# Mixing four paths on VectorE: 32 multiply-and-adds of 64 columns per half batch in place of whole weighings and additions

## The reference, cut to what matters

```
paths = (short, longp, delta, v)
probs = softmax(logits, -1); probs = maximum(probs, floor_val); probs = probs / probs.sum(-1, keepdims=True)
out = sum((probs[..., i, None] * p for i, p in enumerate(paths)))
out = out * rsqrt(mean(out * out, -1, keepdims=True) + 1e-05) * onorm_w
return out.reshape(B, L, -1) @ Wo.T
```

## Time and profile before

| | us |
|---|---|
| median of three runs | 1904.76 |
| profiled execution | 1897.1 |
| its span, first to last instruction | 1895.4 |
| VectorE busy | 1353.1 (71%) |
| TensorE busy | 1501.2 (79%) |
| ScalarE busy | 949.5 (50%) |
| GpSimd busy | 436.7 (23%) |
| mean granted TensorE clock | 0.899 of full speed |

### The profile page before, as it was taken

How to read it: one execution, slowest core, us unless ns; L and a number is a source line. 1 busy time by engine, 2 the same in 40 slices (tenths; PEclk the granted TensorE clock), 3 DMA queues, 4 the chain that set the end, 5 groups by cost and what they waited for, 6 DMA issues and landing times. The chain is left out here.

```text
span 1895.4 us, 40891 instructions
## 1 busy us (share of the span) xinstructions
PE 1501.2 (79%) x12507; PEld 1111.5 (59%) x12508; DVE 1353.1 (71%) x3875; ACT 949.5 (50%) x1998; POOL 436.7 (23%) x473
## 2 busy tenths in 40 slices
PE   6776065979999999999999999997436999999800
PEld 3446034737747657657567477476225888888700
DVE  6996055687798887887887887976455455554488
ACT  6772161356455654654655564542443555555434
POOL 6783200000030040040120310300233333333300
PEclk9997586989999999999999999987657999999955
DMA  5548632023243243333342333332524533333295
GB/s 198 191 161 256 168 72 72 3 58 100 73 119 99 60 124 102 79 90 101 93 117 81 93 100 87 93 101 63 190 99 134 188 105 103 101 105 100 79 384 192
DMA packets 297373, 224.36 MB, mean 118 GB/s; under 512 B 173472, under 2 KB 265632, under 8 KB 296960
## 3 DMA queue, kind: packets, MB, share of 16 engines
q1 hardware_dynamic: 225600, 158.84, 28.9%
q0 software_dynamic: 15232, 43.53, 6.3%
q10 hardware_dynamic: 56384, 19.93, 4.1%
HBM read 130.42 MB, written 91.82 MB: 117 GB/s over the span
## 5 line engine op out<-in xcount | busy, mean ns | idle before, releaser
L2041 POOL DMA_INDIRECT y_d<-C_yb,C_dest x136 | 131.6, 968 | 235.0 <-ACT C_yb L2152 232.6
L1465 DVE SCALAR_TENSOR_TENSOR B_conv<-B_ps_x,B_cw,B_conv 128x511 f32<-128x511 f32 (+2 forms) x192 | 143.4, 747 | 51.9 <-ACT B_conv L1177 46.9
L422 POOL DMA_INDIRECT xs_d<-x,slot_u x128 | 133.3, 1042 | 136.7 <-DVE m_acc L1867 100.0
L688 POOL MEMSET B_z<- 128x256 f32 (+4 forms) x40 | 5.6, 199 | 690.7 <-DMA B_z<-scr_a 690.7
L1177 ACT ACTIVATE B_conv<-B_ps_x,B_cw 128x512 f32<-128x512 f32 x64 | 43.7, 683 | 167.2 <-PE B_ps_x L745 165.9
L2271 DVE TENSOR_TENSOR C_av<-C_sg,C_ps_g 128x256 f32<-128x256 f32 x136 | 57.2, 421 | 95.2 <-ACT C_sg L2146 95.2
L745 PE MATMUL B_ps_x<-B_xa,B_wk 128*128 128x512 f32 x128 | 68.1, 660 | 65.8 <-DVE B_sel L1457 45.0
L2075 PE MATMUL C_ps_g<-C_w_high,C_xt_high 128*128 x272 | 120.0, 441 | 0.3 <-DVE C_xt_low L2277 0.3
L2283 DVE TENSOR_TENSOR C_avt_low<-C_ps_a,C_avt_high 128x256 fp32r<-128x256 f32 x136 | 57.6, 424 | 85.2 <-ACT C_avt_high L2141 85.2
L2075 PE MATMUL C_ps_g<-C_w_high,C_xt_low 128*128 x272 | 108.3, 398 | 0.0
L2075 PE MATMUL C_ps_g<-C_w_low,C_xt_high 128*128 x272 | 107.4, 395 | 0.0
(11 more groups left out here) (334 smaller groups left out, 4274.4 us busy)
## 6 DMA issues: line engine op xcount, KB each, us to landing
C_xb<-xs_d SPq DMA_DIRECT2D x136, 132.0 KB, 2.1
C_w_high<-y_d SPq DMA_DIRECT2D x12, 1024.0 KB, 14.0
A_band<-fir_long POOLq DMA_DIRECT2D x32, 256.0 KB, 5.6
A_work<-xT SPq DMA_DIRECT2D x16, 512.0 KB, 4.9
v_d<-A_v_tok SPq DMA_DIRECT2D x16, 512.0 KB, 3.5
short_d<-A_sh_tok SPq DMA_DIRECT2D x16, 512.0 KB, 3.2
B_xa<-xT SPq DMA_DIRECT2D x8, 1024.0 KB, 5.6
B_v_tok<-v_d SPq DMA_DIRECT2D x8, 1024.0 KB, 5.4
```

What stands on the lines that cost most here:

```text
L422: pool.indirect_dma_start(t["xs_d"][:, :], bass.IndirectOffsetOnAxis(ap=slot_u[:, c:c + 1], axis=0), x1[:, b, j, :], None).then_inc(done, 16)
L1465: V.scalar_tensor_tensor(conv[:, g % 2, k:], X[g % 2][:, :SEQ - k], cw[:, g // 4, gg % CH, 3 - k:4 - k], conv[:, g % 2, k:], ALU.mult, ALU ...
L2041: pool.indirect_dma_start(t["y_d"][:, :], bass.IndirectOffsetOnAxis(ap=dest[:, q:q + 1], axis=0), yb[:, u], None).then_inc(y_out[u], 16)
```

## The change

On VectorE a half batch is now mixed into `lo` in four steps. `weigh` multiplies the long rows as before and then joins the delta rows by 16 instructions, one for each tile and head, each of which computes `lo = rows * p + lo` on 64 columns, with the probability as a scalar per partition. `add_short` does the same with the short rows. `add_value` adds the values, weighed by ScalarE as before, in one 128 x 1024 addition. Gone are the multiplications of `delta` and `sh`, and the additions of `delta` to `lo`, of the values to `sh` and of `sh` to `lo` (the addition of the values to `lo` stands in their place). `add_value` of half 1 comes ahead of `sum_squares` of half 0; `add_rest` of half 1 came behind `scale_mix` of half 0. The semaphore `mixd` is gone, and `load_v` waits for the finished mix of both halves. The counts of `mix` stay as they were.

```diff
                 def load_v(i):
-                    hold(sp, mixd, 4 * i)
+                    for k in mix:
+                        hold(sp, k, 7 * i - 3)
                     sp.dma_start(v_tok[:], tok("v_d")[:, bass.ds(i * PT, PT), :]).then_inc(v_in, 16)
...
+                def add_weighed(i, b, rows, k):
+                    for j in range(TPB):
+                        for h in range(HEADS):
+                            n_, hs = b * TPB + j, slice(h * DH, (h + 1) * DH)
+                            w = V.scalar_tensor_tensor(lo[:, b, j, hs], rows[:, j, hs],
+                                                       lg[:, n_ * HEADS + h, k:k + 1], lo[:, b, j, hs],
+                                                       ALU.mult, ALU.add)
+                    w.then_inc(mix[b], 1)
                 def weigh(i, b):
...
                     dve.wait_ge(sm_dve, 11 * (i + 1))
-                    V.tensor_tensor(v3(lo[:, b]), v3(lo[:, b]), p3(1), ALU.mult).then_inc(mix[b], 1)
-                    V.tensor_tensor(v3(dlt), v3(dlt), p3(2), ALU.mult).then_inc(mix[b], 1)
-                    V.tensor_tensor(v3(sh[:, b]), v3(sh[:, b]), p3(0), ALU.mult).then_inc(mixd, 1)
-                def add_two(i, b):
+                    V.tensor_tensor(v3(lo[:, b]), v3(lo[:, b]), long_p, ALU.mult).then_inc(mix[b], 1)
+                    dve.wait_ge(mix[b], 7 * i + 1)
+                    add_weighed(i, b, delta[:, b * TPB:(b + 1) * TPB], 2)
+                def add_short(i, b):
                     dve.wait_ge(mix[b], 7 * i + 2)
-                    V.tensor_tensor(lo[:, b], lo[:, b], delta[:, b * TPB:(b + 1) * TPB], ALU.add).then_inc(mix[b], 1)
-                    val = v_tok[:, b * TPB:(b + 1) * TPB]
-                    dve.wait_ge(mixd, 2 * (2 * i + b) + 1)
+                    add_weighed(i, b, sh[:, b], 0)
+                def add_value(i, b):
+                    dve.wait_ge(mix[b], 7 * i + 3)
                     dve.wait_ge(weighed, 2 * i + b + 1)
-                    V.tensor_tensor(sh[:, b], sh[:, b], val, ALU.add).then_inc(mixd, 1)
-                def add_rest(i, b):
-                    dve.wait_ge(mix[b], 7 * i + 3)
-                    dve.wait_ge(mixd, 2 * (2 * i + b + 1))
-                    V.tensor_tensor(lo[:, b], lo[:, b], sh[:, b], ALU.add).then_inc(mix[b], 1)
+                    V.tensor_tensor(lo[:, b], lo[:, b], v_tok[:, b * TPB:(b + 1) * TPB], ALU.add).then_inc(mix[b], 1)
...
                         merge(i + 1, 0)
-                    add_two(i, 0)
-                    add_rest(i, 0)
+                    add_short(i, 0)
+                    add_value(i, 0)
                     if has_next:
                         merge(i + 1, 1)
                     weigh(i, 1)
                     if has_next:
                         merge(i + 1, 2)
-                    add_two(i, 1)
+                    add_short(i, 1)
+                    add_value(i, 1)
                     sum_squares(i, 0)
                     if has_next:
                         merge(i + 1, 3)
                     scale_mix(i, 0)
-                    add_rest(i, 1)
                     sum_squares(i, 1)
```

More of the change, by code:

```diff
@@ L514, in delta_and_gate @@
         sm_dve, sm_exp = sem("softmax_dve"), sem("softmax_exp")
-        weighed, mixd, mix = sem("values_weighed"), sem("mix_rest"), [sem(f"mix_dve{i}") for i in range(2)]
+        weighed, mix = sem("values_weighed"), [sem(f"mix_dve{i}") for i in range(2)]
         sq_ok, rms_rt = sem("rms_squared"), sem("rms_rooted")
@@ L1724, in weigh @@
                 def weigh(i, b):
-                    p3 = lambda k: lg[:, 16 * b:16 * b + 16, k:k + 1].to_broadcast([P, 16, DH])
-                    dlt = delta[:, b * TPB:(b + 1) * TPB]
+                    long_p = lg[:, 16 * b:16 * b + 16, 1:2].to_broadcast([P, 16, DH])
                     dve.wait_ge(sm_dve, 11 * (i + 1))
-                    V.tensor_tensor(v3(lo[:, b]), v3(lo[:, b]), p3(1), ALU.mult).then_inc(mix[b], 1)
-                    V.tensor_tensor(v3(dlt), v3(dlt), p3(2), ALU.mult).then_inc(mix[b], 1)
```

## The result

| | before | after |
|---|---|---|
| median of the runs, us | 1902.93 (4 runs) | 1928.93 (4 runs) |
| ratio to before, 95% interval | | 1.0144 (1.0116 to 1.0172) |
| profiled execution, us | 1897.1 | 1928.5 |
| span, us | 1895.4 | 1926.8 |
| VectorE busy, us | 1353.1 | 1388.5 |

The two profiled executions lie 31.4 us apart: the one of the kernel before is 6 us faster than the median of its runs, the other at its median.

The account below looks back on a forecast made before the run. VectorE was taken to set the end of a pair's mixing, with TensorE waiting. Seven pairs at 2.4 us plus 2.6 in the last gave +19 on 1904.8: 1924 us, by itself 1916 to 1932, all cases 1908 to 1940.

Parts of the forecast that it names:

- The instruction: VectorE's added 64-column multiply-and-adds start 0.195 us apart, sixteen last 3.2 us; +1.7 us of work per half batch.
- The rule of the Trainium skill: 58 cycles plus columns at 0.96 GHz, 127 ns for 64 columns; weighed against 0.195 us, it would give the faster rival's sum.
- The weighing of half 0, hidden in the gap: VectorE's first weighing grows to 4.46 us, cost 0: hidden by 1.0 of the 1.63 us gap ahead of the taps.
- Short rows of half 0 behind GpSimd's masking: On VectorE, the first short-row multiply-and-add waits for GpSimd's masking to end, as the long addition did; cost +0.9 us.
- The order gives back the wait for the square: On VectorE, the 1.12 us wait ahead of the second sum of squares goes; reordering gives back 2.3 of 4.0 us.
- `first_rows` waits about 0.7 us for the load: Values' load lands 4.0 us later, at 864.3; VectorE reaches `first_rows` at 863.6 and waits about 0.7 us.
- L937 moves by 2.4 us a pair: TensorE's L937, behind `first_rows` and merge 4 at the mixing's end, moves from 863.92 to 866.3: +2.4 us.
- The last pair: No merges, no load, no gap hiding the first weighing: its second sum of squares comes 2.6 us later.
- TensorE in between, at no cost: TensorE's L929 starts 2.2 us later and ends at 864.4, in time for merge 4: cost 0.
- The clock: Rival, 12%: another stretch at TensorE's lower clock after new idling, 1.7 us a pair, 12 us more: 1936 us.
- The last rival: 10%: half or more of the step meets slack in the recurrence, where VectorE waits for TensorE's products: 1905 to 1914.

Follow-up runs that it names:

- the run with a constant: The changed kernel with the constant 0.25 in place of each row's probability in the 64-column multiply-and-adds: 1893.66 us, ratio 0.9934 to the kernel before.
- the order alone: The kernel before with its instructions kept and half 1's last addition moved ahead of half 0's sum of squares: 1887.57 us, ratio 0.9911.
- the instructions alone: The changed kernel in the old order, half 1's values added behind the scaling of half 0: 1953.1 us, ratio 1.0294 to the kernel before.
- the values first: The changed kernel with half 1's values added ahead of its short rows, the next values' load waiting for that addition alone: by itself 1923.86 us, ratio 1.0104.
- the first filler alone: The changed kernel with two more TensorE filler products ahead of L930, VectorE's program untouched: 1925.35 us, ratio 1.0098 to the kernel before.

## Why the prediction was right, and where its sum fell short

*The instruction* (forecast 0.195 us apart, 3.2 us for sixteen): right, 0.196 and 3.22. The whole cost hung on choosing the row of the same operation with a scalar per partition over the row of equally short statistics; the run with a constant shows that this scalar is what sets the two apart. The rule of the Trainium skill ("VectorE: DVE Perf Modes", section on the TRN2 errata) that was weighed there, by which 64 columns are an estimate of 127 ns, is met by the constant's 0.136 us more nearly than by the 0.196 us of this kernel.

*The weighing of half 0, hidden in the gap:* right, 1.63 became 0.57. *Short rows of half 0 behind GpSimd's masking:* right, the call at 854.85 takes 4.21 us, 1.0 more than elsewhere. The masking in that mixing:

```profile
852.21 3.83 POOL L699 TENSOR_SCALAR_AFFINE_SELECT area<-area 128x4096 f32<-128x4096 f32 x1 [12.43 <-DMA area<-scr_xt]
```

In the first pair the masking (GpSimd, below) falls into the delta rows' call (VectorE) instead:

```profile
433.93 3.98 POOL L699 TENSOR_SCALAR_AFFINE_SELECT area<-area 128x4096 f32<-128x4096 f32 x1 [35.80 <-DMA area<-scr_xt]
```
```profile
431.12 6.87 DVE L1730 SCALAR_TENSOR_TENSOR B_lo<-B_delta,B_lg,B_lo 128x64 f32<-128x64 f32 x16
```

6.87 us in place of 3.22. The prediction did not look at where the masking lies in that pair. In the kernel before it starts 4.2 us behind the mixing's start there (437.98 - 433.82), 6.1 in the pair that was followed. VectorE's busy time grew by 35 us where 27 were forecast; the held call is 3.7 us of that.

*The order gives back the wait for the square:* right, and confirmed from both sides by the order alone and the instructions alone. *`first_rows` waits about 0.7 us for the load:* right, 0.73. *L937 moves by 2.4 us a pair:* 2.52 in the pair that was followed, but there luck helped: the other six moved by 3.1 to 6.2 us, and the seven by 3.8 on average. *The last pair:* right, its second sum of squares comes 2.46 us later after the mixing's start (20.85 us against 18.39), where 2.6 were forecast.

*TensorE in between, at no cost:* this is the step that failed, a term of the sum put at 0. The prediction saw L929 start 2.2 us late (2.38 measured, 873.65 - 846.14 against 858.31 - 833.18) and counted it as covered because VectorE was later still. The idling was followed by a longer stretch at 1.2 GHz, some 10 us in place of 3.4 in that pair: L930 itself grew from 3.94 to 5.71 us, which the prediction had at 3.94. In the profiled executions, the parts from `first_rows` on are 5.6 + 8.3 = 13.9 us over seven mixings, where the sum has 0. The part up to `first_rows` is 20.8 us, where the sum has 7 x 2.4 = 16.8; 2.3 of those 4.0 us more come from the first pair. The clock was a rival of its own at 12%, with 12 us on top of the sum, and the median of 1928.93 lies between the forecast, 1924, and that rival, 1936. The median fell into the range although the term is missing from the sum. How the 26 us between the medians divide was not measured; the 13.9 us hold for the two profiled executions, of which the one before is a fast one.

*The last rival,* slack further on, goes the other way: the recurrence did not take up time but lost 1.5 us more in the pair that was followed and 8.3 us over seven, at the lower clock.

## What to carry to other kernels

Many short instructions on VectorE pay their rest each time, here 68 ns, and 128 ns where each reads a scalar per partition; price them by a row of the same operation with the same kind of scalar, not by their columns. When time is added to one engine, look at which other engine it leaves idle, and price that idling too where the idle engine's clock can fall. Split a change into its order and its instructions before judging it: here the order alone was worth 0.9% and was hidden under the instructions' 2.9%.

## What the runs showed of the hardware that was not expected

- Some 60 ns of a VectorE multiply-and-add belong to its scalar per partition (0.196 against 0.136 us apart at 64 columns).
- Two filler products (1.9 us) at each of the two places where TensorE idled about 2 us, and the values first, raise the mean granted clock of the runs from between 0.887 and 0.890 to between 0.903 and 0.906; the kernel before has 0.891 to 0.902. With the first filler alone, the same program ran at either 0.890 to 0.891 or 0.895 to 0.900, 10 to 16 us apart.
- A stretch of 3.4 us at 1.2 in place of 2.4 GHz behind the mixing made the same hundred microseconds of work about 1.3 us longer (101.3 to 102.6 us on average over twelve kernels), a stretch of 6.8 us about 2.4 us longer (103.7).
- Multiply-and-adds of 64 columns that read two SBUF tensors are held by GpSimd's masking as long additions are: sixteen took 6.87 us in place of 3.22.
